# Attention scores in eight tiles of 32 rows by 64 columns with one buffer, in a decoder layer on one core

## The reference

```python
x = x + self_attention(layernorm(x))                  # 16 heads of 8, causal
x = x + cross_attention(layernorm(x), ctx)            # 16 heads of 8, biases, then an MLP 128-256-128
z = layernorm(x)
h = z + rotary_attention(rmsnorm(z, g1))              # 16 heads of 8, causal, rotary
x = x + h + moe(rmsnorm(h, g2))                       # 8 experts, top 2, hidden 384
# attention, for each sequence and head:
scores = einsum('bhqd,bhkd->bhqk', q, k) * 8 ** -0.5  # (-inf where k > q, if causal)
out = einsum('bhqk,bhkd->bhqd', softmax(scores), v)
```

## Time and profile before

| what | value |
|---|---|
| median of three runs | 782.73 us (779.57 to 784.61) |
| the profiled execution, its own time | 776.94 us |
| its span, first to last instruction | 775.1 us |
| mean granted TensorE clock | 0.935 |
| TensorE busy (matmuls) | 633.1 us, 82% of the span |
| VectorE busy | 501.8 us, 65% |
| ScalarE busy | 393.4 us, 51% |
| GpSimd busy | 270.5 us, 35% |
| first and last scores start at | 23.6 us and 505.4 us |

### The profile page before, as it was taken

The page is one execution under the profiler, slowest core; times in us unless marked ns, Lnnn a source line. Parts: engine busy times, 40 slices in busy tenths (PEclk is TensorE's granted clock), DMA queues, the critical chain, the costliest instruction groups (busy, mean ns, idle before and its releaser), DMA issues. The chain is left out here.

```text
span 775.1 us, 26457 instructions
## 1 busy us (share of the span) xinstructions
PE 633.1 (82%) x10869; PEld 453.5 (59%) x10869; DVE 501.8 (65%) x1131; ACT 393.4 (51%) x831; POOL 270.5 (35%) x391
## 2 busy tenths in 40 slices
PE   3899999999899889989987797952359988898840
PEld 1466666665565555555554554641359988888840
DVE  5578886767676775867666575846926655454537
ACT  4455565655455545563544425433527765565525
POOL 6001010202111321412304232220857777777750
PEclk9899999999999999999999999995559999999985
DMA  4407201000000010111100100100041111111129
GB/s 114 119 17 234 53 21 26 17 26 17 16 26 17 15 53 3 26 43 27 43 17 7 38 16 16 58 37 20 2 142 47 56 52 53 52 52 54 52 74 296
DMA packets 36774, 39.75 MB, mean 51 GB/s; under 512 B 11792, under 2 KB 26960, under 8 KB 36528
## 3 DMA queue, kind: packets, MB, share of 16 engines
q1 hardware_dynamic: 32112, 28.74, 12.1%
q0 software_dynamic: 4544, 9.32, 4.2%
HBM read 20.80 MB, written 10.94 MB: 41 GB/s over the span
## 5 line engine op out<-in xcount | busy, mean ns | idle before, releaser
L1071 ACT ACTIVATE probsT<-ring 128x512 f32<-128x512 f32 x192 | 103.7, 591 | 124.7 <-PE ring L1020 124.6
L1191 DVE TENSOR_REDUCE rmax<-ps_s 128x16 f32<-128x1024 f32 x96 | 116.8, 1217 | 61.5 <-PE ps_s L1008 61.5
L1195 DVE TENSOR_TENSOR shifted<-ps_s,rmax 128x1024 f32<-128x1024 f32 x96 | 117.6, 1225 | 9.9
L657 PE MATMUL ps_s<-room 128*128 128x128 f32 x852 | 109.4, 279 | 0.0
L1020 PE MATMUL ring<-const,shifted 128*128 128x128 f32 x768 | 106.9, 283 | 0.8 <-DVE att L1206 0.8
L657 PEld LDWEIGHTS ps_s<-room 128*128 128x128 f32 x852 | 103.1, 196 | 0.0
L1008 PE MATMUL ps_s<-room,qT 64*64 64x512 f32 x768 | 101.5, 603 | 0.0
L1036 PEld LDWEIGHTS ring<-vbd,probsT 128*32 128x32 f32 x6144 | 63.0, 111 | 52.4 <-issue 46.6
L735 DVE SCALAR_TENSOR_TENSOR room<-room,ps_s 128x384 f32<-128x384 f32 x71 | 39.3, 554 | 81.0 <-ACT room L707 81.0
L1020 PEld LDWEIGHTS ring<-const,shifted 128*128 128x128 f32 x768 | 84.2, 143 | 4.2 <-DVE shifted L1195 0.9
L602 POOL DMA_INDIRECT room<-hn_dram,gather_rows x71 | 68.8, 969 | 28.9 <-issue 20.4
(11 more groups left out here) (172 smaller groups left out, 919.7 us busy)
## 6 DMA issues: line engine op xcount, KB each, us to landing
room<-kS SPq DMA_DIRECT2D x192, 32.0 KB, 1.9
room<-y_dram SPq DMA_DIRECT2D x16, 256.0 KB, 6.0
room<-in_x SPq DMA_DIRECT2D x8, 256.0 KB, 3.5
hn_dram<-hn SPq DMA_DIRECT2D x8, 256.0 KB, 2.3
base_dram<-base SPq DMA_DIRECT2D x8, 256.0 KB, 2.4
room<-base_dram SPq DMA_DIRECT2D x1, 2048.0 KB, 8.0
out<-room SPq DMA_DIRECT2D x8, 256.0 KB, 4.5
cin<-in_ctx SPq DMA_DIRECT2D x8, 192.0 KB, 3.4
```

The source lines that it names most:

```text
L657: last = mm(bank[r][:, k * P:(k + 1) * P], w, xbT[r], start=True, stop=True)
L1071: nc.scalar.activation(probsT[p % 2][:, 4 * g:4 * g + 4, :], ring[u.bank][:].rearrange("p (k c) -> p k c", c=P), ACT.Exp, scale=SCALE)\
L1191: V.reduce_max(rmax[p % 2][:], ps_s[p % 2][:], AX.X).then_inc(rmax_ready, 1)
L1195: V.tensor_tensor(shifted[p % 2][:], ps_s[p % 2][:], rmax[p % 2][:].unsqueeze(2).broadcast_to([P, HEADS, SEQ]), ALU.subtract)\
```

## The change

The heads are in four groups of four, each group in 32 partitions, and a pair's scores are eight matmuls, 32 rows by 64 columns of the array with 256 columns each. Each of the four groups writes the first half of a PSUM bank of its own (`banks`), so one pair takes the same four banks that two pairs had, and there is no second buffer: `scores` waits for the shift of the previous pair. The mask is written by eight matmuls of 256 columns, which still take 64 rows by 64 columns. The keys are spread by four DMAs of twice the size for a job, and the cleared key tiles are half as large. The weight columns and the rotary tables follow the new order of heads. In `walk` VectorE's `shift` of the following pair stands ahead of the steps of place 0, among them drains of `q`, `ff` and `kr`. For a rotary job `ap` writes `xh` alone; `fres` is written by a step of its own, `ap3`, in the last round (place 1) of the job two before, with its own semaphore, for which `wo`'s drain and the factor computations wait. The first scores come after `setup_rotated`, since both use the same PSUM.

```diff
+SLOTS = 4
+GROUPS = HEADS // SLOTS
+ROWS = P // GROUPS
...
-        ROTARY: (((), ("st",)), (("ap",), ()), (("xT",), ("k",)), (("kr",), ()))},
+        ROTARY: (((), ("st",)), (("ap",), ()), (("xT",), ("k",)), (("kr",), ("ap3",)))},
...
             if following[0] < N_JOBS:
                 scores(*following)
+                shift(*following)
             steps(steps_at(n, p, 0))
-            if following[0] < N_JOBS:
-                shift(*following)
...
-    ps_s = [ctx.enter_context(nc.psum_tensor(f"ps_s{r}", [P, HEADS, SEQ], F32)) for r in range(2)]
+    banks = ctx.enter_context(nc.psum_tensor("ps_s", [P, GROUPS, 512], F32))
+    ps_s = banks[:, :, 0:SLOTS * SEQ].rearrange("p g (k s) -> p g k s", k=SLOTS)
...
-            for k in range(HALF):
-                sp.dma_start(kbd[r][k:P:HALF, k, :], kS[r][k:P:HALF, :]).then_inc(kbd_loaded[r], 16)
+            for k in range(SLOTS):
+                sp.dma_start(kbd[r][k:P:SLOTS, k, :], kS[r][k:P:SLOTS, :]).then_inc(kbd_loaded[r], 16)
...
-            wait(pe, centered, pair - 1)
+            wait(pe, centered, pair)
             if causal:
+                for j in range(GROUPS // 2):
+                    for q in range(2):
+                        for b in range(2):
+                            g, rows, half_rows = 2 * q + j, slice(SEQ * b, SEQ * b + SEQ), slice(SEQ * q, SEQ * q + SEQ)
+                            mm(ps_s[rows, g], identb[half_rows, half_rows],
+                               maskb[half_rows, :].unsqueeze(1).broadcast_to([SEQ, SLOTS, SEQ]), start=True, stop=False)
...
+            for b in range(2):
                 tok = (2 * p + b) * SEQ
-                last = mm(ps_s[half][rows, HALF * g:HALF * g + HALF, :], qT[r][half_rows, tok:tok + SEQ],
-                          kbd[r][half_rows, :, tok:tok + SEQ], start=not causal, stop=True)
+                for g in range(GROUPS):
+                    some = slice(ROWS * g, ROWS * g + ROWS)
+                    last = mm(ps_s[SEQ * b:SEQ * b + SEQ, g], qT[r][some, tok:tok + SEQ], kbd[r][some, :, tok:tok + SEQ],
+                              start=not causal, stop=True)
...
+        setup_rotated()
         scores(0, 0)
-        setup_rotated()
...
-            V.reduce_max(rmax[p % 2][:], ps_s[p % 2][:], AX.X).then_inc(rmax_ready, 1)
+            V.reduce_max(rmax[p % 2][:].rearrange("p (g k) -> p g k", g=GROUPS), ps_s, AX.X).then_inc(rmax_ready, 1)
...
+        def apply_third(n):
+            m, t = NORMS["st", n], TILE_OF[n]
+            r = m % 2
+            for s in range(SUB):
+                last = nc.scalar.activation(fres[t % 4][:, s, :], xs[t][:, s, :], ACT.Identity,
                                             bias=shift[r][:, 0, s:s + 1], scale=rstd[r][:, s:s + 1])
+            last.then_inc(third_rows, 1)
...
                 elif name == "wo" and kind == ROTARY:
                     wait(dve, base_ready, t)
+                    dve.wait_ge(third_rows, t + 1)
...
             wait(pool, normed, m - 2)
+            wait(pool, third_rows, THIRDS[m - 2])
```

More of the change, by code:

```diff
@@ L70, in slot_row @@
     h, d = divmod(c, D)
-    return h // HALF * SEQ + d * HALF + h % HALF
+    return h // SLOTS * ROWS + d * SLOTS + h % SLOTS
 def by_slot(w):
-    return w.rearrange("p (g k d) -> p g d k", g=2, d=D)
+    return w.rearrange("p (g k d) -> p g d k", g=GROUPS, d=D)
 def in_slots(w):
-    return w.rearrange("p (g d k) -> p g d k", g=2, d=D)
+    return w.rearrange("p (g d k) -> p g d k", g=GROUPS, d=D)
 def constants():
@@ L98, in constants @@
     emb = np.concatenate([freqs, freqs], axis=-1)
-    c[:, C_COS:C_COS + SEQ] = np.tile(np.repeat(np.cos(emb).T, HALF, axis=0), (2, 1))
-    c[:, C_SIN:C_SIN + SEQ] = np.tile(np.repeat(np.sin(emb).T, HALF, axis=0), (2, 1))
+    c[:, C_COS:C_COS + SEQ] = np.tile(np.repeat(np.cos(emb).T, SLOTS, axis=0), (GROUPS, 1))
+    c[:, C_SIN:C_SIN + SEQ] = np.tile(np.repeat(np.sin(emb).T, SLOTS, axis=0), (GROUPS, 1))
     q, k = np.arange(P)[:, None] % SEQ, np.arange(SEQ)[None, :]
@@ L143 @@
 }
-NOT_ON_PE = ("st", "ap", "st2", "ap2")
+NOT_ON_PE = ("st", "ap", "ap3", "st2", "ap2")
 def steps_at(n, p, place):
@@ L228 @@
 USES, NORMS = count_uses()
+THIRDS = {m: 0 for m in range(-1, len(NORMS) + 1)}
+for (name, n), m in NORMS.items():
+    if name == "st" and KIND_OF[n] == ROTARY:
+        THIRDS[m] = TILE_OF[n] + 1
 N_USES = len(USES)
@@ L295, in _build @@
     rope = room[1][:, HALF * TILE:(HALF + 4) * TILE].rearrange("p (k t) -> p k t", k=4)
-    kbd = [room[r][:, 0:HALF * TILE].rearrange("p (h t) -> p h t", h=HALF) for r in range(2)]
+    kbd = [room[r][:, 0:SLOTS * TILE].rearrange("p (h t) -> p h t", h=SLOTS) for r in range(2)]
     vbd = [sb(f"vbd{r}", [P, 2 * SUB * VW]) for r in range(2)]
@@ L385, in _build @@
     normed = sem("normed")
+    third_rows = sem("third_rows")
     b2_added = sem("b2_added")
@@ L557, in there @@
         return 0 <= i * UNROLL + c < USED
-    g_bank = [ps_s[0][:].rearrange("p h k -> p (h k)")[:, 512 * r:512 * r + HIDDEN] for r in range(2)]
-    u_bank = [ps_s[1][:].rearrange("p h k -> p (h k)")[:, 512 * r:512 * r + HIDDEN] for r in range(2)]
+    g_bank = [banks[:, r, 0:HIDDEN] for r in range(2)]
+    u_bank = [banks[:, 2 + r, 0:HIDDEN] for r in range(2)]
     x_bank = ps_o[:, 0:P]
@@ L882, in _ @@
         mm = nc.tensor.matmul
-        setup = ps_s[1][:].rearrange("p h k -> p (h k)").rearrange("p (k c) -> p k c", c=P)
+        setup = banks[:, 2, :].rearrange("p (k c) -> p k c", c=P)
         def setup_first():
@@ L989, in scores @@
         def scores(n, p):
-            pair, r, half = n * SUB + p, n % 2, p % 2
+            pair, r = n * SUB + p, n % 2
             causal = KIND_OF[n] != CROSS
-            wait(pe, centered, pair - 1)
-            tiles = [(g, b, slice(SEQ * g, SEQ * g + SEQ), slice(SEQ * b, SEQ * b + SEQ))
-                     for g in range(2) for b in range(2)]
+            wait(pe, centered, pair)
             if causal:
-                for g, b, half_rows, rows in tiles:
-                    mm(ps_s[half][rows, HALF * g:HALF * g + HALF, :], identb[half_rows, half_rows],
-                       maskb[half_rows, :].unsqueeze(1).broadcast_to([SEQ, HALF, SEQ]), start=True, stop=False)
+                for j in range(GROUPS // 2):
[4 more added lines that the diff above has]
+                               maskb[half_rows, :].unsqueeze(1).broadcast_to([SEQ, SLOTS, SEQ]), start=True, stop=False)
             if p == 0:
-                pe.wait_ge(kbd_loaded[r], 16 * HALF * (n // 2 + 1))
+                pe.wait_ge(kbd_loaded[r], 16 * SLOTS * (n // 2 + 1))
                 if KIND_OF[n] == ROTARY:
@@ L1079, in apply @@
             r = m % 2
[L1080 to L1083, removed]
             for s in range(SUB):
-                dst = fres[t % 4] if kind == ROTARY else xh
-                last = nc.scalar.activation(dst[:, s, :], xs[t][:, s, :], ACT.Identity,
+                bias = shift[r][:, 1 if kind == ROTARY else 0, s:s + 1]
+                scale = (rboth if kind == ROTARY else rstd)[r][:, s:s + 1]
+                last = nc.scalar.activation(xh[:, s, :], xs[t][:, s, :], ACT.Identity, bias=bias, scale=scale)
+            last.then_inc(normed, 1)
+        def apply_third(n):
[3 more added lines that the diff above has]
+                last = nc.scalar.activation(fres[t % 4][:, s, :], xs[t][:, s, :], ACT.Identity,
                                             bias=shift[r][:, 0, s:s + 1], scale=rstd[r][:, s:s + 1])
-            last.then_inc(normed, 1)
+            last.then_inc(third_rows, 1)
         def apply_rms(n):
@@ L1113, in use @@
                 apply_rms(n)
-            if name in ("st", "ap", "st2", "ap2", "wo", "ff", "lg", "qr", "kr") or (kind == ROTARY and name in ("q", "k")):
+            elif name == "ap3":
+                apply_third(n)
+            if name in ("st", "ap", "ap3", "st2", "ap2", "wo", "ff", "lg", "qr", "kr") or (kind == ROTARY and name in ("q", "k")):
                 return
@@ L1120, in use @@
             if name == "k":
-                wait(act, kbd_loaded[r], 16 * HALF * (n // 2))
+                wait(act, kbd_loaded[r], 16 * SLOTS * (n // 2))
             act.wait_ge(ring_filled, u.filled())
@@ L1157, in _ @@
         act.wait_ge(setup_filled, 1)
-        given = ps_s[1][:].rearrange("p h k -> p (h k)")[:, 0:4 * P].rearrange("p (k c) -> p k c", c=P)
+        given = banks[:, 2, :].rearrange("p (k c) -> p k c", c=P)
         for k in range(2):
@@ L1164, in _ @@
         act.wait_ge(weights_loaded, 16 * N_LOADS)
-        turned = ps_s[1][:].rearrange("p h k -> p (h k)")[:, 0:2 * P].rearrange("p (k c) -> p k c", c=P)
+        turned = banks[:, 2, 0:2 * P].rearrange("p (k c) -> p k c", c=P)
         act.wait_ge(setup_filled, 2)
-        nc.scalar.activation(bias_qk[:], ps_s[1][:, 4, 0:2], ACT.Copy)
+        nc.scalar.activation(bias_qk[:], banks[:, 2, 2 * P:2 * P + 2], ACT.Copy)
         nc.scalar.activation(w_turned[:], turned, ACT.Copy).then_inc(setup_drained, 1)
@@ L1194, in shift_scores @@
```

(9 more changed lines are left out.)

3 lines of the change are left out of this document (1 added, 2 removed).

## The result

The changed kernel takes 758.17 us (757.28 to 758.55, four runs), the kernel before 783.23 us beside it; the ratio is 0.9685 (95% interval 0.9651 to 0.972). A later comparison of the same two gave 757.52 and 0.9689 (0.9647 to 0.973). The prediction was 756.5 us within 744 to 777.

A forecast was written before the change was run, and what follows sets the result against it. TensorE was taken to bound the first attention jobs, TensorE and waits the later rotary ones. Terms +4.6 + 2.7 - 23.7 - 9.1 + 2.0 - 3.0 = -26.5 us, against 782.73, gave 756.5 us; range 744 to 777.

The forecast's parts named there:

- Scores in eight tiles: TensorE's scoring stage: eight tiles side by side shorten it from 0.96 to 0.52 us, 0.43 us less; bounds 0 and 0.48.
- the slower rival: Scoring stage: 32-row tiles overlap no further than 64-row ones, giving 795 us; chance 0.10.
- the rival of a partial one: Scoring stage: partial overlap saves 0.30 us a stage (or a change of form costs 0.3 us), 767 us; chance 0.20.
- The new change of form: Between mask and scores in causal kinds: one more change of tile form costs 0.09 us; bounds 0 and 0.4.
- The 63 rounds' -23.7 us: Rounds still limited by TensorE: 38 before causal scores gain 0.34 us each, 25 before cross scores 0.43.
- The single buffer: Scores wait for the previous pair's shift: no round shorter than 3.35 us, or 3.68 before causal scores; +4.6 us.
- The 19 rounds: Of the 91 rounds, those whose length the single buffer's loop decides: +4.6 us in sum.
- VectorE's rounds: Nine rounds cannot fall under VectorE's work plus 0.25 us for hand-overs: +2.7 us in all.
- Rotary rows and clock: Rotary preparation: `xh` without `fres` gains 1.1 us eight times, -9.1 us with rounding; fewer half-clock stretches, -3 us.
- Shift ahead of the drains: VectorE's order: shift earlier, banks returned 2.6 us later, `q`'s wait about 0.9 us already counted; nothing more.
- Prologue: Start of the kernel: setup before first scores, second scores at 29.95 us against 28.06; +2.0 us.

The follow-up runs named there:

- experiment 9: experiment 4's kernel with the mask written in the scores' own form, 16 instead of 8 mask instructions: 748.98 us, ratio 0.9576.
- experiment 10: experiment 4's kernel with the experts' weights loaded in job 6 instead of job 1: 754.91 us, ratio 0.9658.
- experiment 3: Kernel before with `ap3`, the shift ahead of the drains and scores waiting for the previous pair's shift, still 64-row tiles: 770.54 us, ratio 0.9873.
- experiment 2: Kernel before with `ap3` and the shift ahead of the drains, still two score buffers and 64-row tiles: 758.50 us, ratio 0.9710.
- experiment 1: Kernel before with only `fres` moved to its own step `ap3`: 764.44 us, ratio 0.9798.
- experiment 6: Changed kernel with the shift back behind the drains: 774.38 us, ratio 0.9922.
- experiment 4: Changed kernel with the setup in the fourth ring bank, so the first scores come ahead of it: 754.24 us, ratio 0.9666.
- experiments 9 to 11: experiment 9, experiment 10, and experiment 9's kernel with the five experts' weight loads one to a job in jobs 1 to 5: 750.33 us, ratio 0.9595.
- experiments 3 to 11: Include, otherwise unnamed: changed kernel again, 757.52 us; with `fres` back in `apply`, 778.36 us; with that and the shift back behind the drains, 796.10 us.

## Why the prediction was right, point by point

The time and the sign were right; the sum in the traces was 18.7 us against 26.5 forecast, and the match of the medians (25.1) has some luck in it, since the sum was made against a quick execution of before. By its own steps, over the same rounds:

- **Scores in eight tiles.** All eight run side by side, so the slower rival is out. In the row at 38.37 the first eight instructions start within 0.05 us, and the second of a tile starts 0.27 us after the first, where it was 0.43; without the change of form (experiment 9) it is 0.22, as forecast for full overlap, so the rival of a partial one is out too. In cross rounds the stage went from 1.02 to 0.62 us; in causal ones, from 0.96, it saves 0.34 us with the new change of form ahead of it and 0.42 without (0.54, experiment 9), against 0.43.
- **The new change of form** was mis-sized: 0.17 us in a causal round by experiment 9, not 0.09. It lies in two places, the way from mask to scores (0.24 to 0.35 us) and the first step of the scores. The 63 rounds' -23.7 us was -18.8 in those 55 of them without a rotary preparation, where -20.5 was forecast; the stop of experiment 10 is in that number with about 2 us. By the Trainium skill's drain (TensorEngine Tiling (Array Packing), Key Properties), priced at the full latency of 0.15 us, I would have been nearer. The runs agree that a change of form costs TensorE time; that it is a drain no row shows.
- **The single buffer.** The loop was forecast at 3.68 and 3.35 us and is 3.75 and 3.41. Its parts in the round at 38.37: scores to reduction 0.80 us (0.68 forecast), reduction and subtraction 2.55 (as forecast), from there to the mask 0.05 (0.12, for which I had no row), mask to scores 0.35 (0.33). The 19 rounds lost 6.9 us against 4.6, 1 us of it at the stop. The count of the rounds that the loop decides was right to the round (experiment 3).
- **VectorE's rounds**: +1.9 against +2.7, and that it comes so near is luck, for VectorE did not set them. Two that I had at +0.8 each (from 4.37 us) became 0.24 us shorter. Five grew from 4.7 to 4.8 us to 5.1 to 5.5, but there TensorE waits for the late drain of `q`, a cost of the shift's place:

```profile
212.27 1.10 PE L994 MATMUL ring<-xT,w_f 128*128 128x512 f32 x2 [0.56 <-DVE room L1284]
```

  With the same order and the old tiles four of these five last 5.48 us (experiment 2), so the tiles gave 0.36 us there, where I had said that TensorE's gain is worth nothing.
- **Rotary rows and clock.** The eight rounds were forecast at -9.1 for the rows, -3.2 for the tiles in them and -3 for the clock, 15.3 in all; they gained 13.6 us. The three half-clock stretches went, but a new one came (259.5 to 262.9 us) in a round that is 0.6 us longer than before; in experiment 1 the same round was 1.5 us shorter. Alone, on the kernel before, the step gives 16.3 us there (experiment 1), and 20 us when taken out of the changed kernel. This term was mis-sized as a term of its own: I cut the 1.5 us a round to 1.1 to share it with other terms.
- **Shift ahead of the drains** I cost at nothing. This step failed. Beside two buffers it gave 6 to 7 us by medians and ratios (experiment 2), of which the traces show 2.9 us as its own balance; with the single buffer it is worth 16 to 18 us (experiment 6), since every drain ahead of the shift lies in the loop. The wait for `q`'s drain was forecast at 0.9 us and is 0.56 to 0.65.
- **Prologue.** This step failed too: "+2.0 us" was +5.7. I had the second scores at 29.95 us; they came at 31.63, and the next pair 6.1 us later than before, with the clock at half to 37.6 us instead of 25.5. I had counted the work of the prologue at full speed. With the old order experiment 4 had the clock up at 25.6 us and made up all of the 5.7 us; experiments 9 to 11, with the clock up at 33.2 to 33.6, more than half.
- **The stop in `attend`** (about 3 us) was in no step.

Where the gain lies is another matter than the sum suggested. The chain of versions by ratio: before 1; `ap3` 0.980; shift first 0.971; single buffer 0.987; tiles 0.967; the prologue's order 0.9685 (the whole change). The tiles' 16 us pay for their single buffer (12 to 13) and their prologue (2 to 4) and leave next to nothing: 0.971 (0.9685 to 0.9734) without them, 0.9685 (0.9651 to 0.972) with them. The change is fast because of the two edits of order, and these need no tiles; but on the single buffer they are necessary.

Left open: how much of the medians' difference between versions 1 and 2 is the shift's place and how much the clock; why the stop in `attend` comes with the load in some versions and not in others; what the tiles would give with two buffers, which was not tried (with four groups in four banks, the second buffer would have to lie in the other halves of the same banks).

## What to carry to other kernels

When an edit takes a buffer away to make a stage shorter, write down the loop that it closes and count the rounds shorter than that; then ask what the other edits of the same change would do without it. A queue worked in order hides its cost in the first piece that others wait for: split such a step and let the part nobody waits for go behind. Two tile forms next to each other can be worth making one even at the price of twice the instructions: here it gave 6 us.

## What the runs showed of the hardware

- Float32 matmuls of 32 rows by 64 columns with 256 columns run eight side by side: at full clock sixteen of 373 to 425 ns take 0.69 us, and 0.61 where the mask ahead of them has their form.
- Between the mask (64 by 64) and the scores (32 by 64) a change of form costs 0.17 us a round (0.15 in rounds that the loop decides).
- The order of work in the prologue goes with the length of its half-clock stretch: with the first scores behind the setup it lasted 17.1 us in all five traces, with them ahead of it 6.8 to 13.7 us in eight. In the changed kernel it ended at 37.6 instead of 25.5 us, and the round of pair 0.1 took 6.74 us instead of 4.21.
- While 1.5 to 4.5 MB are loaded into the weights' tile, TensorE's issue can stop: for 1.6 to 3.0 us in experiments 3 to 11, and the stop moved with the load (experiment 10). Before and the kernels of experiments 1 and 2 had the same load and no stop over 0.6 us.
